# Causal attention weighed in gangs of four heads, one chunk at a time into four PSUM quadrants

## The chip, the cores and the metric

The kernel runs on one core of a Trainium2 chip. The metric is the device time of one execution in microseconds. It uses five engines: TensorE (PE; its weight loads are PEld), VectorE (DVE), ScalarE (ACT), GpSimd (POOL), and SyncE (SP), which issues the DMAs. TensorE's clock is granted at one of two levels, 1.2 or 2.4 GHz, which the profile shows as 0.5 and 1.0.

## The reference

The input is `x` of 8 x 512 x 128 in float32. Four blocks with residuals follow each other: causal attention with ALiBi (16 heads of 8 channels), a gated feed-forward network of 384 hidden channels, a second attention that works on selected and compressed keys, and the same feed-forward network again.

```python
# first attention, per sample: x is 512 x 128, 16 heads of 8
qkv = layernorm(x) @ w_qkv.T + b_qkv
scores = einsum('bhqd,bhkd->bhqk', q, k) / sqrt(8)
scores = scores + where(k <= q, -(q - k), -1e30)
probs = softmax(scores, axis=-1)
out = einsum('bhqk,bhkd->bhqd', probs, v)
x = x + out @ w_out.T + b_out
x = x + (silu(h @ wg.T) * (h @ wu.T)) @ wd.T          # h = layernorm(x), weights int32 / 127
# second attention: full 512 x 512 softmax per head gives the importance of each token
#   (entropy, maximum, influence); 51 tokens are gathered, 64 groups of 8 are compressed;
#   the 115 keys and values of each head are then attended to
x = x + attention_b(layernorm(x)) ; x = x + ffn(layernorm(x))
```

The change is in the line `out = einsum(...)` of the first attention and in the exponentials ahead of it.

## The kernel before, in words

The eight samples go through a pipeline of passes, `one_pass(i, a, p, m, s)`. In one pass four stages work on different samples side by side: `p` projects queries, keys and values of sample i+1; `a` is the causal attention and feed-forward network of sample i; `m` computes the full softmax of the second attention of sample i-1 and selects its keys; `s` attends with the small key set and runs the last feed-forward network of sample i-2. There are eleven passes. The first has `p` alone; the next has `a` and `p`; the next `a`, `p` and `m`; five in a hardware loop have all four; one has all but `p`; two more drain the pipeline. The causal attention `a` is in eight of them, in six of these beside both `m` and `s`. Each pass ends in a barrier of all engines.

Inside a pass the order of every engine's instructions is written out by hand in steps `n` from 0 to 74. In each of the first 64 steps `m` takes one 128 x 512 tile of the full scores: PE multiplies (`full_scores`, issued one step ahead), DVE finds the maximum (L947), ACT exponentiates (L747) and takes a logarithm (L750), POOL computes a threshold (L606), DVE sums an entropy two steps later (L902), and DVE or ACT scales the probabilities six steps later (L919, L693), which POOL adds up (L580).

The changed part of `a` stands in steps 20 to 49 (`A2_AT` to `A2_END`). Its scores are recomputed with the row maximum subtracted, transposed: keys in partitions, queries in columns. A head has four key tiles of 128; their widths are 512, 384, 256 and 128 because of causality, and they are packed into three units (`TILES`, `WIDTH`): one of 512, one of 384 + 128, one of 256. So there are 48 units `u` in a pass, in the steps that `a2_tiles(n)` gives, five units in every three steps. For each unit PE writes the scores and a mask into bank 3 or 4 alternately (`causal_minus_max`, L1165 and L1167), ACT takes the exponential into the probability buffer `pT` (L776), and PE multiplies the probabilities with the head's eight value columns and a column of ones (`weigh`, L1183). That product has nine rows; it goes to the quadrant of bank 5 that belongs to the head modulo four (`QROWS` 32, `HPQ` 4). A matmul in float32 is two records in the profile. After four heads ACT copies bank 5 out (`leave`, L686) and PE transposes it (`turn`, L1216). Unit `u` = 3 x head + chunk: one head's three chunks, then the next head's. `weigh(u - 3)` follows `causal_minus_max(u)`.

The small second attention has the same form: `weigh_hh` (L1197) writes head after head into the quadrants of bank 5, sometimes two heads in one step. The full scores (L1229) read partitions 64 and up of the same stacks from which the causal scores read the lower ones.

Of the kernel before, what the change touches and what calls it, by code (L numbers as in the profile page):

```python
# [9 lines left out]
BF16 = mybir.dt.bfloat16  # L10
# [3 lines left out]
P = 128  # L14
# [8 lines left out]
def hybrid_block(nc, x, w_qkv, b_qkv, w_out, b_out, wq_b, wk_b, wv_b, wo_b, w_gate, w_up, w_down, out):  # L23
    B, T, D = x.shape
# [15 lines left out]
    AL = 4  # L40
# [8 lines left out]
    with ExitStack() as ctx:  # L49
# [56 lines left out]
        kst = [k_stacks[64 * s:64 * s + 64, :, :] for s in range(2)]  # L106
        nm = [sb(f"nm{s}", [P, NT, H]) for s in range(2)]
        qsm = sb("qsm", [64, H, T], BF16)
        nmf = [sb(f"nmf{s}", [H, T]) for s in range(2)]
        nmr = [sb(f"nmr{s}", [H, T]) for s in range(2)]  # L110
        nmp = [sb(f"nmp{s}", [H, 3, T], BF16) for s in range(2)]
        vA = sb("vA", [P, NT, H, HD + 1])
        pT = [sb(f"pT{i}", [P, sum(WIDTH)]) for i in range(2)]
        ov = sb("ov", [P, T])
        rzo = [sb(f"rzo{s}", [P, NT, 4]) for s in range(2)]
        o = [sb(f"o{s}", [P, NT, P]) for s in range(2)]
# [25 lines left out]
        vrden = sb("vrden", [L, H])  # L142
        NE = 8
        E = setup[:, :].rearrange("p (n t) -> p n t", n=NE)
        alibi = sb("alibi", [1, AL + 1, T], BF16)
        junk = sb("junk", [P, T])
        nmB = sb("nmB", [P, H, NT])
        Z = sb("Z", [P, H, NT])
# [287 lines left out]
        def a1_before(u):  # L436

            return max([v + 1 for v in range(u) if a1_bank(v) == a1_bank(u)], default=0)

        def a2_tiles(n):  # L440

            return [u for u in range(3 * H) if A2_AT + (3 * u) // 5 == n]
# [19 lines left out]
        def one_pass(i, a, p, m, s):  # L462
            with nc.Block() as block:
# [176 lines left out]
                def _(act):  # L640
# [37 lines left out]

                    def leave(k, g):

                        act.wait_ge(s_pv[k], HPQ * (g + 1) * (1 if k else 3))
                        if g:
                            act.wait_ge(s_tv[k], g)
                        elif k == 0 and s:
                            act.wait_ge(s_tv[1], H // HPQ)
                        act.activation(ov[:, :], bank[5][:, :], ACT.Copy).then_inc(s_ov[k], 1)  # L686
# [51 lines left out]
                    for n in range(STEPS):  # L738
# [26 lines left out]
                        if a:  # L765
                            if n == S2_AT:
                                max_high(0)
                            if n == S2_AT + 2:
                                max_mid(0)

                            for u in a2_tiles(n):
                                h, c = u // 3, u % 3
                                if h >= 2:
                                    act.wait_ge(s_pv[0], u - 5)
                                act.wait_ge(s_s2[0], u + 1)
                                act.activation(pT[h % 2][:, c * T:c * T + WIDTH[c]], bank[3 + u % 2][:, 0:WIDTH[c]],  # L776
                                               ACT.Exp).then_inc(s_p[0], 1)
                        if m:

# [58 lines left out]
                def _(dve):  # L838
# [103 lines left out]
                    for n in range(STEPS):  # L942
# [159 lines left out]
                        if p:  # L1102
# [5 lines left out]
                            if n == P_TAIL + 7:  # L1108

                                dve.wait_ge(s_proj[0], 3)  # L1110
                                if a:
                                    dve.wait_ge(s_pv[0], 3 * H)
                                for t in range(NT):
                                    last = dve.tensor_tensor(
                                        vA[:, t, :, 0:HD],
                                        bank[5][:, t * P:(t + 1) * P].rearrange("p (h d) -> p h d", d=HD),
                                        bv[:, :].rearrange("p (h d) -> p h d", d=HD), ALU.add)
                                last.then_inc(s_vt[0], 1)

                @block.tensor  # L1120
                def _(pe):
# [33 lines left out]
                        last.then_inc(s_mt[k], 1)  # L1155

                    def causal_minus_max(u):
                        h, parts = u // 3, TILES[u % 3]
                        if u >= 2:
                            pe.wait_ge(s_p[0], u - 1)  # L1160
                        elif s:
                            pe.wait_ge(s_p[1], H)
                        for k, at in parts:
                            w = T - k * P
                            pe.matmul(bank[3 + u % 2][:, at:at + w], kst[0][0:A_MX, h, k * P:(k + 1) * P],  # L1165
                                      qst[0][0:A_MX, h, k * P:T], start=True, stop=True)
# [1 line left out]
                                             start=False, stop=True, skip_group_check=True)  # L1168
                        last.then_inc(s_s2[0], 1)

                    def weigh(u):

                        h, c = u // 3, u % 3
                        pe.wait_ge(s_p[0], u + 1)
                        if h >= HPQ and h % HPQ == 0:
                            pe.wait_ge(s_ov[0], h // HPQ)
                        if h == 0 and s:
                            pe.wait_ge(s_ov[1], H // HPQ)
                        elif h == 0:
                            pe.wait_ge(s_ma[0], 1)  # L1180
                        q = QROWS * (h % HPQ)
                        for k, at in TILES[c]:
                            last = pe.matmul(bank[5][q:q + HD + 1, k * P:T], vA[:, k, h, :],  # L1183
                                             pT[h % 2][:, c * T + at:c * T + at + T - k * P], start=(k == 0),
                                             stop=True, skip_group_check=(k > 0))
                        last.then_inc(s_pv[0], 1)

                    def weigh_hh(h):
# [113 lines left out]
                    for n in range(STEPS):  # L1302
# [123 lines left out]
                        if a:  # L1426
                            if n == A2_AT:
                                pe.wait_ge(s_mrow[0], DMA)
                            for u in a2_tiles(n):
                                causal_minus_max(u)  # L1430
                                if u > 2:
                                    weigh(u - 3)
                            if n == A2_END:
                                for u in range(3 * H - 3, 3 * H):
                                    weigh(u)
                            if n in TURN_AT[0]:
                                turn(0, TURN_AT[0].index(n))
                            if n == A_TAIL:
# [75 lines left out]
```

## Time and profile before

| | |
|---|---|
| median of 3 runs | 2352.26 us (2349.68 to 2664.49) |
| span of the profiled execution | 2347.5 us, 25009 instructions |
| PE busy | 1731.0 us, 74% |
| DVE busy | 1492.3 us, 64% |
| ACT busy | 1121.6 us, 48% |
| POOL busy | 892.7 us, 38% |
| DMA, main queue | 57.57 MB, 15.1% of 16 engines |
| L1183, weighing | 1024 records |
| L776, exponentials | 384 |

The profiled execution has no time of its own beside its span, which lies 2.2 us below the fastest run and 4.8 us below the median. Busy time is a sum over stages with different limits, so the share of the whole span says little; the rows below are by stage. In the timeline a record's length includes a part in which the next record already runs, so the time that an operation holds PE is read from its start to the start of what follows.

### The profile page before, as it was taken

The numbers are of one execution on the slowest core, as the hardware profiler recorded it, in microseconds if no ns is written. First come the engines' busy times: TensorE is split into PE (matmuls) and PEld (weight loads), VectorE is DVE, ScalarE is ACT, GpSimd is POOL, SyncE is SP. The second block draws the span as 40 slices with busy tenths as digits, with TensorE's granted clock in tenths as the row PEclk, the third lists the DMA queues.
The fourth block names the chain that finished last, engine by engine and source line by source line (L and its number), as shares of the span: only waits on it lengthen the run. The fifth ranks groups of instructions, "written<-read, shape, count | busy, mean of one in ns | idle before, by whom it ended". The sixth has DMA issues, their size and how long they took to land. (4 is left out here: it accounts for less than half of the span.)

```text
span 2347.5 us, 25009 instructions
## 1 busy us (share of the span) xinstructions
PE 1731.0 (74%) x6733; PEld 734.6 (31%) x6733; DVE 1492.3 (64%) x3701; ACT 1121.6 (48%) x2726; POOL 892.7 (38%) x1252
## 2 busy tenths in 40 slices
PE   1686479668986799568976799668977799647537
PEld 1222233333333332333334332433334332322122
DVE  0401388847886677757875677757876677647931
ACT  1033167516772277416672376516672377446603
POOL 2001146513553155514562154514562155425700
PEclk9998559756987599756987589756987589656557
DMA  3002300250004200240005100240005100130010
GB/s 61 13 2 37 53 2 1 38 75 4 1 5 87 29 3 1 50 69 4 1 12 84 24 3 1 46 72 4 1 5 90 20 3 1 24 51 1 5 24 5
DMA packets 64106, 59.35 MB, mean 25 GB/s; under 512 B 10400, under 2 KB 61648, under 8 KB 63952
## 3 DMA queue, kind: packets, MB, share of 16 engines
q1 hardware_dynamic: 63952, 57.57, 15.1%
q8 instruction: 63, 1.03, 0.2%
q14 instruction: 91, 0.75, 0.1%
HBM read 39.10 MB, written 18.27 MB: 24 GB/s over the span
## 5 line engine op out<-in xcount | busy, mean ns | idle before, releaser
L580 POOL TENSOR_TENSOR psum<-psum,setup 128x512 f32<-128x512 f32 x480 | 614.1, 1279 | 55.5 <-ACT setup L693 52.1
L947 DVE TENSOR_REDUCE nmB<-bank 128x1 f32<-128x512 f32 x512 | 348.2, 680 | 290.7 <-PE bank L1229 289.8
L747 ACT ACTIVATE setup<-bank,nmB 128x512 f32<-128x512 f32 x512 | 349.8, 683 | 283.4 <-DVE nmB L947 252.7
L606 POOL TENSOR_TENSOR thr<-lnZ,nmB 128x1 f32<-128x1 f32 x512 | 102.1, 199 | 790.3 <-ACT lnZ L750 786.9
L902 DVE SCALAR_TENSOR_TENSOR junk<-bank,thr,setup 128x512 f32<-128x512 f32 x512 | 378.6, 739 | 20.5 <-POOL thr L606 18.8
L1229 PE MATMUL bank<-k_stacks,q_stacks 48*128 48x512 bf16 x512 | 236.8, 470 | 181.1 <-DMA k_stacks<-part_dram 111.0
L1183 PE MATMUL bank<-pT,vA 128*9 128x512 f32 (+3 forms) x1024 | 342.4, 440 | 10.8 <-ACT ov L686 10.6
L866 DVE TENSOR_REDUCE nm<-bank 128x1 f32<-128x512 f32 (+3 forms) x512 | 225.6, 482 | 127.6 <-PE bank L1148 124.7
L1145 PE MATMUL bank<-k_stacks,q_stacks 52*128 52x512 bf16 (+3 forms) x512 | 217.4, 425 | 120.0 <-PEq L1476 59.2
L776 ACT ACTIVATE pT<-bank 128x512 f32<-128x512 f32 (+1 forms) x384 | 198.8, 521 | 190.9 <-PE bank L1167 188.8
L919 DVE TENSOR_SCALAR setup<-setup,rz 128x512 f32<-128x512 f32 x288 | 195.0, 677 | 0.0
L1229 PEld LDWEIGHTS bank<-k_stacks,q_stacks 48*128 48x128 bf16 x512 | 47.7, 96 | 418.5 <-DVE junk L902 167.7
L1165 PE MATMUL bank<-q_stacks,k_stacks 55*128 55x512 bf16 (+3 forms) x512 | 159.8, 312 | 21.4 <-ACT pT L776 11.9
L1148 PE MATMUL bank<-maskqk,identb 128*128 128x128 bf16 x512 | 143.3, 280 | 0.0
L693 ACT ACTIVATE setup<-setup,rz 128x512 f32<-128x512 f32 x192 | 135.6, 706 | 0.0
L1197 PE MATMUL bank<-p,vsm 115*9 115x512 f32 x256 | 124.6, 722 | 4.4 <-ACT ov L686 3.6
L1167 PE MATMUL bank<-maskkq,identb 128*128 128x128 bf16 x512 | 118.6, 232 | 0.0
L750 ACT ACTIVATE lnZ<-Z 128x1 f32<-128x1 f32 x512 | 103.9, 203 | 16.2
L875 DVE RECIPROCAL rzo<-bank 128x16 f32<-128x16 f32 x64 | 16.3, 254 | 146.6 <-PE bank L1216 146.6
L1145 PEld LDWEIGHTS bank<-k_stacks,q_stacks 52*128 52x128 bf16 x512 | 51.9, 101 | 182.4 <-issue 90.9
L763 ACT ACTIVATE p<-bank 115x512 f32<-115x512 f32 x128 | 72.2, 584 | 66.5 <-PE bank L1397 33.8
L747 ACT ACTIVATION_READ_ACCUMULATOR setup<-bank,nmB 128x1 f32 x512 | 101.7, 199 | 0.0
(184 smaller groups left out, 2370.5 us busy)
## 6 DMA issues: line engine op xcount, KB each, us to landing
part_dram<-part SPq DMA_DIRECT2D x16, 768.0 KB, 3.3
q_stacks<-part_dram SPq DMA_DIRECT2D x96, 128.0 KB
k_stacks<-part_dram SPq DMA_DIRECT2D x96, 128.0 KB
qsm<-part_dram SPq DMA_DIRECT2D x48, 128.0 KB
x<-in_L_attn_a_x_dram SPq DMA_DIRECT2D x8, 256.0 KB, 3.9
x_dram<-x SPq DMA_DIRECT2D x8, 256.0 KB, 10.2
x2s<-x_dram SPq DMA_DIRECT2D x8, 256.0 KB, 11.4
out_dram<-x SPq DMA_DIRECT2D x8, 256.0 KB, 2.3
```

What stands on the lines that cost most here:

```text
L580: pool.tensor_tensor(psum[:, :], psum[:, :], E[:, n % NE, :], ALU.add).then_inc(s_bi, 1)
L747: act.activation(E[:, n % NE, :], RING[n % RN][:, :], ACT.Exp, bias=nmB[:, h, t:t + 1], accum_out=Z[:, h, t:t + 1]).then_inc(s_be, 1)
L776: act.activation(pT[h % 2][:, c * T:c * T + WIDTH[c]], bank[3 + u % 2][:, 0:WIDTH[c]], ACT.Exp).then_inc(s_p[0], 1)
L866: last = dve.tensor_reduce(nm[0][:, t, h:h + 1], bank[a1_bank(u)][:, at:at + (t + 1) * P], AX_X, ALU.max, negate=True)
L902: dve.scalar_tensor_tensor(out=junk[:, :], in0=RING[n % RN][:, :], scalar=thr[:, h, t:t + 1], in1=E[:, n % NE, :], op0=ALU.max, op1=ALU.mu ...
L919: dve.tensor_scalar(E[:, n % NE, :], E[:, n % NE, :], rz[:, h, t:t + 1], None, ALU.mult).then_inc(s_scv, 1)
L947: dve.tensor_reduce(nmB[:, h, t:t + 1], RING[n % RN][:, :], AX_X, ALU.max, negate=True).then_inc(s_bm, 1)
L1145: pe.matmul(bank[a1_bank(u)][:, at:at + (t + 1) * P], qst[0][0:A_SC, h, t * P:(t + 1) * P], kst[0][0:A_SC, h, 0:(t + 1) * P], start=True, ...
L1148: last = pe.matmul(bank[a1_bank(u)][:, at + t * P:at + (t + 1) * P], identb[:, :], maskqk[:, :], start=False, stop=True, skip_group_check= ...
L1165: pe.matmul(bank[3 + u % 2][:, at:at + w], kst[0][0:A_MX, h, k * P:(k + 1) * P], qst[0][0:A_MX, h, k * P:T], start=True, stop=True)
L1183: last = pe.matmul(bank[5][q:q + HD + 1, k * P:T], vA[:, k, h, :], pT[h % 2][:, c * T + at:c * T + at + T - k * P], start=(k == 0), stop=T ...
L1229: pe.matmul(RING[n % RN][:, :], qst[1][0:B_SC, h, t * P:(t + 1) * P], kst[1][0:B_SC, h, :], start=True, stop=True).then_inc(s_bs, 1)
```

## The change

Unit `u` now stands for another tile. `gang_tile(u)` gives head `4 * (u // 12) + u % 4` and chunk `u // 4 % 3`: the first chunk of four heads, then the second chunk of the four, then the third. There are four probability buffers instead of two, one for each head of a gang. A weighing unit is now a chunk of a gang (12 in a pass instead of 48): for each key tile of the chunk four matmuls, one for each quadrant of bank 5, then one increment of the semaphore. All waits on it are rescaled. To make room, the two maxima buffers `nmf` and `nmr` are shared between the two attentions, and the constant rows `alibi` lie in the setup tile.

```diff
--- before.py
+++ after.py
@@ -106,11 +106,11 @@
         kst = [k_stacks[64 * s:64 * s + 64, :, :] for s in range(2)]
         nm = [sb(f"nm{s}", [P, NT, H]) for s in range(2)]
         qsm = sb("qsm", [64, H, T], BF16)
-        nmf = [sb(f"nmf{s}", [H, T]) for s in range(2)]
-        nmr = [sb(f"nmr{s}", [H, T]) for s in range(2)]
+        nmf = [sb("nmf", [H, T])] * 2
+        nmr = [sb("nmr", [H, T])] * 2
         nmp = [sb(f"nmp{s}", [H, 3, T], BF16) for s in range(2)]
         vA = sb("vA", [P, NT, H, HD + 1])
-        pT = [sb(f"pT{i}", [P, sum(WIDTH)]) for i in range(2)]
+        pT = [sb(f"pT{i}", [P, sum(WIDTH)]) for i in range(4)]
         ov = sb("ov", [P, T])
         rzo = [sb(f"rzo{s}", [P, NT, 4]) for s in range(2)]
         o = [sb(f"o{s}", [P, NT, P]) for s in range(2)]
@@ -142,7 +142,7 @@
         vrden = sb("vrden", [L, H])
         NE = 8
         E = setup[:, :].rearrange("p (n t) -> p n t", n=NE)
-        alibi = sb("alibi", [1, AL + 1, T], BF16)
+        alibi = setup[0:1, 22 * P:].bitcast(BF16).rearrange("p (a t) -> p a t", a=AL + 1)
         junk = sb("junk", [P, T])
         nmB = sb("nmB", [P, H, NT])
         Z = sb("Z", [P, H, NT])
@@ -437,6 +437,10 @@
 
             return max([v + 1 for v in range(u) if a1_bank(v) == a1_bank(u)], default=0)
 
+        def gang_tile(u):
+
+            return HPQ * (u // (3 * HPQ)) + u % HPQ, u // HPQ % 3
+
         def a2_tiles(n):
 
             return [u for u in range(3 * H) if A2_AT + (3 * u) // 5 == n]
@@ -678,7 +682,7 @@
 
                     def leave(k, g):
 
-                        act.wait_ge(s_pv[k], HPQ * (g + 1) * (1 if k else 3))
+                        act.wait_ge(s_pv[k], (g + 1) * (HPQ if k else 3))
                         if g:
                             act.wait_ge(s_tv[k], g)
                         elif k == 0 and s:
@@ -769,11 +773,11 @@
                                 max_mid(0)
 
                             for u in a2_tiles(n):
-                                h, c = u // 3, u % 3
-                                if h >= 2:
-                                    act.wait_ge(s_pv[0], u - 5)
+                                h, c = gang_tile(u)
+                                if h >= HPQ:
+                                    act.wait_ge(s_pv[0], u // HPQ - 2)
                                 act.wait_ge(s_s2[0], u + 1)
-                                act.activation(pT[h % 2][:, c * T:c * T + WIDTH[c]], bank[3 + u % 2][:, 0:WIDTH[c]],
+                                act.activation(pT[h % HPQ][:, c * T:c * T + WIDTH[c]], bank[3 + u % 2][:, 0:WIDTH[c]],
                                                ACT.Exp).then_inc(s_p[0], 1)
                         if m:
 
@@ -1109,7 +1113,7 @@
 
                                 dve.wait_ge(s_proj[0], 3)
                                 if a:
-                                    dve.wait_ge(s_pv[0], 3 * H)
+                                    dve.wait_ge(s_pv[0], 3 * H // HPQ)
                                 for t in range(NT):
                                     last = dve.tensor_tensor(
                                         vA[:, t, :, 0:HD],
@@ -1155,12 +1159,12 @@
                         last.then_inc(s_mt[k], 1)
 
                     def causal_minus_max(u):
-                        h, parts = u // 3, TILES[u % 3]
+                        h, c = gang_tile(u)
                         if u >= 2:
                             pe.wait_ge(s_p[0], u - 1)
                         elif s:
                             pe.wait_ge(s_p[1], H)
-                        for k, at in parts:
+                        for k, at in TILES[c]:
                             w = T - k * P
                             pe.matmul(bank[3 + u % 2][:, at:at + w], kst[0][0:A_MX, h, k * P:(k + 1) * P],
                                       qst[0][0:A_MX, h, k * P:T], start=True, stop=True)
@@ -1168,21 +1172,21 @@
                                              start=False, stop=True, skip_group_check=True)
                         last.then_inc(s_s2[0], 1)
 
-                    def weigh(u):
-
-                        h, c = u // 3, u % 3
-                        pe.wait_ge(s_p[0], u + 1)
-                        if h >= HPQ and h % HPQ == 0:
-                            pe.wait_ge(s_ov[0], h // HPQ)
-                        if h == 0 and s:
+                    def weigh(w):
+
+                        g, c = w // 3, w % 3
+                        pe.wait_ge(s_p[0], HPQ * (w + 1))
+                        if c == 0 and g:
+                            pe.wait_ge(s_ov[0], g)
+                        elif c == 0 and s:
                             pe.wait_ge(s_ov[1], H // HPQ)
-                        elif h == 0:
+                        elif c == 0:
                             pe.wait_ge(s_ma[0], 1)
-                        q = QROWS * (h % HPQ)
                         for k, at in TILES[c]:
-                            last = pe.matmul(bank[5][q:q + HD + 1, k * P:T], vA[:, k, h, :],
-                                             pT[h % 2][:, c * T + at:c * T + at + T - k * P], start=(k == 0),
-                                             stop=True, skip_group_check=(k > 0))
+                            for j in range(HPQ):
+                                last = pe.matmul(bank[5][QROWS * j:QROWS * j + HD + 1, k * P:T], vA[:, k, HPQ * g + j, :],
+                                                 pT[j][:, c * T + at:c * T + at + T - k * P], start=(k == 0),
+                                                 stop=True, skip_group_check=(k > 0))
                         last.then_inc(s_pv[0], 1)
 
                     def weigh_hh(h):
@@ -1428,11 +1432,10 @@
                                 pe.wait_ge(s_mrow[0], DMA)
                             for u in a2_tiles(n):
                                 causal_minus_max(u)
-                                if u > 2:
-                                    weigh(u - 3)
+                                if u >= HPQ and u % HPQ == 1:
+                                    weigh(u // HPQ - 1)
                             if n == A2_END:
-                                for u in range(3 * H - 3, 3 * H):
-                                    weigh(u)
+                                weigh(3 * H // HPQ - 1)
                             if n in TURN_AT[0]:
                                 turn(0, TURN_AT[0].index(n))
                             if n == A_TAIL:
```

PE in the middle of the stage, pass of the hardware loop, before. `pT` are probability buffers, `vA` values; `k_stacks` and `q_stacks` hold the parts of keys and queries; bank 5 collects the weighed heads, banks 0, 1, 2 and 6 take full scores.

```order
L1165 MATMUL bank3<-q_stacks,k_stacks 128x512 [waits probabilities0]
L1167 MATMUL bank3<-maskkq,identb 128x128
L1183 MATMUL bank5<-pT1,vA 9x512 [waits probabilities0]
L1229 MATMUL bank6<-k_stacks,q_stacks 128x512 [waits entropy_sums]
L1165 MATMUL bank4<-q_stacks,k_stacks 128x384 [waits probabilities0]
L1167 MATMUL bank4<-maskkq,identb 128x128
L1165 MATMUL bank4<-q_stacks,k_stacks 128x128
L1167 MATMUL bank4<-maskkq,identb 128x128
L1183 MATMUL bank5<-pT1,vA 9x384 [waits probabilities0]
L1183 MATMUL bank5<-pT1,vA 9x128
L1165 MATMUL bank3<-q_stacks,k_stacks 128x256 [waits probabilities0]
L1167 MATMUL bank3<-maskkq,identb 128x128
```

The same place after the change:

```order
L1233 MATMUL bank2<-k_stacks,q_stacks 128x512 [waits entropy_sums]
L1169 MATMUL bank4<-q_stacks,k_stacks 128x384 [waits probabilities0]
L1171 MATMUL bank4<-maskkq,identb 128x128
L1169 MATMUL bank4<-q_stacks,k_stacks 128x128
L1171 MATMUL bank4<-maskkq,identb 128x128
L1187 MATMUL bank5<-pT0,vA 9x512 [waits four_heads_out_of_psum0,probabilities0]
L1187 MATMUL bank5<-pT1,vA 9x512
L1187 MATMUL bank5<-pT2,vA 9x512
L1187 MATMUL bank5<-pT3,vA 9x512
L1233 MATMUL bank6<-k_stacks,q_stacks 128x512 [waits entropy_sums]
L1169 MATMUL bank3<-q_stacks,k_stacks 128x384 [waits probabilities0]
L1171 MATMUL bank3<-maskkq,identb 128x128
```

One head's weighing stood behind each unit of scores. Now four heads' weighing stands together behind the second of four units of scores; the three units between have none.

ACT at the same steps, before:

```order
L747 ACTIVATE setup,Z<-bank1,nmB 128x512 [waits influences,entropy_sums,full_maxima]
L750 ACTIVATE lnZ<-Z 128x1 [waits full_exponentials]
L776 ACTIVATE pT1<-bank4 128x256 [waits scores_minus_max0,heads_weighted0]
L747 ACTIVATE setup,Z<-bank2,nmB 128x512 [waits influences,entropy_sums,full_maxima]
L750 ACTIVATE lnZ<-Z 128x1 [waits full_exponentials]
L776 ACTIVATE pT0<-bank3 128x512 [waits scores_minus_max0,heads_weighted0]
L776 ACTIVATE pT0<-bank4 128x512 [waits scores_minus_max0,heads_weighted0]
```

and after:

```order
L751 ACTIVATE setup,Z<-bank1,nmB 128x512 [waits influences,entropy_sums,full_maxima]
L754 ACTIVATE lnZ<-Z 128x1 [waits full_exponentials]
L780 ACTIVATE pT1<-bank4 128x512 [waits scores_minus_max0,heads_weighted0]
L751 ACTIVATE setup,Z<-bank2,nmB 128x512 [waits influences,entropy_sums,full_maxima]
L754 ACTIVATE lnZ<-Z 128x1 [waits full_exponentials]
L780 ACTIVATE pT2<-bank3 128x512 [waits scores_minus_max0,heads_weighted0]
L780 ACTIVATE pT3<-bank4 128x512 [waits scores_minus_max0,heads_weighted0]
```

The exponentials stand in the same steps between those of the full scores; their buffer, and at some places their width, differ.

## Rows read from the trace of the kernel before

**Rows 1.** The page, part 2: granted clock of TensorE, tenths of full speed, 40 slices

```profile
PEclk9998559756987599756987589756987589656557
```

**Rows 2.** Busy time by stage: start:end, length, each engine (x instructions), clock, DMA

```profile
123.90:192.80 68.90, 67.86 (x258) 20.51 (x259) 1.53 (x6) 26.46 (x51) 0.00 (x0) 1.00 0.00 1
344.50:412.10 67.60, 66.03 (x280) 20.16 (x281) 55.26 (x125) 49.55 (x135) 42.11 (x59) 0.96 0.00 1
1116.90:1195.40 78.50, 74.58 (x313) 24.58 (x313) 62.05 (x138) 56.23 (x143) 40.82 (x59) 1.00 0.00 1
1382.40:1463.80 81.40, 77.49 (x313) 24.78 (x314) 61.99 (x139) 56.24 (x143) 40.78 (x59) 0.96 0.00 1
```

**Rows 3.** Waits in 1116.9 to 1195.4: who waited for whom, us, times, longest

```profile
DVE nmB L947 <- PE bank L1229: 13.3, 14, 2.3
```

**Rows 4.** Busy time by stage of line L1183, the weighing, alone

```profile
1116.90:1195.40 78.50, 39.35 (x119) 7.27 (x120) 1.00 0.00 1
```

**Rows 5.** Timeline of PE: start us, length us, instruction, tiles; high clock, full pass

```profile
1144.57 1.03 PE L1183 MATMUL bank<-pT,vA 128*9 128x512 f32 x2
...
1145.53 0.33 PE L1165 MATMUL bank<-q_stacks,k_stacks 55*128 55x384 bf16 x1
...
1146.33 1.03 PE L1183 MATMUL bank<-pT,vA 128*9 128x384 f32 x4
1147.29 0.39 PE L1229 MATMUL bank<-k_stacks,q_stacks 48*128 48x512 bf16 x1
...
1147.77 0.60 PE L1183 MATMUL bank<-pT,vA 128*9 128x256 f32 x2
1148.30 0.39 PE L1165 MATMUL bank<-q_stacks,k_stacks 55*128 55x512 bf16 x1
```

**Rows 6.** Timeline of PE, weighing L1197 of the other attention, low and high clock

```profile
1090.62 1.88 PE L1197 MATMUL bank<-p,vsm 115*9 115x512 f32 x4
1092.44 0.60 PE L1229 MATMUL bank<-k_stacks,q_stacks 48*128 48x512 bf16 x1
...
1095.24 1.03 PE L1197 MATMUL bank<-p,vsm 115*9 115x512 f32 x2
1096.20 0.39 PE L1229 MATMUL bank<-k_stacks,q_stacks 48*128 48x512 bf16 x1
...
1099.30 1.16 PE L1197 MATMUL bank<-p,vsm 115*9 115x512 f32 x4
1100.40 0.66 PE L1216 MATMUL bank<-identf,ov 128*128 128x128 f32 x4
```

**Rows 7.** Timeline of ACT, the probabilities that L1197 weighs

```profile
1098.32 1.06 ACT L763 ACTIVATE p<-bank 115x512 f32<-115x512 f32 x2
```

**Rows 8.** Timeline of PE in the first attention pass, low clock

```profile
125.65 0.60 PE L1165 MATMUL bank<-q_stacks,k_stacks 55*128 55x512 bf16 x1
...
126.41 1.88 PE L1183 MATMUL bank<-pT,vA 128*9 128x512 f32 x2
128.22 0.50 PE L1165 MATMUL bank<-q_stacks,k_stacks 55*128 55x384 bf16 x1
...
129.31 1.88 PE L1183 MATMUL bank<-pT,vA 128*9 128x384 f32 x4
...
131.66 1.02 PE L1183 MATMUL bank<-pT,vA 128*9 128x256 f32 x2
132.62 0.61 PE L1165 MATMUL bank<-q_stacks,k_stacks 55*128 55x512 bf16 x1
```

**Rows 9.** Busy time by stage, with the granted clock (PEclk)

```profile
1051.00:1083.00 32.00, 28.19 (x103) 12.03 (x102) 27.28 (x66) 14.18 (x39) 7.73 (x14) 0.50 0.02 4
1098.00:1116.00 18.00, 14.64 (x52) 3.89 (x51) 11.74 (x31) 17.76 (x44) 11.38 (x16) 1.00 0.01 2
1181.00:1219.00 38.00, 30.22 (x126) 13.69 (x125) 29.64 (x82) 27.16 (x65) 21.81 (x32) 0.96 0.03 8
1199.80:1206.60 6.80, 3.13 (x15) 1.25 (x13) 6.77 (x17) 2.23 (x8) 4.49 (x6) 1.00 0.00 0
```

## The prediction

> **What bounds the kernel now.** I read the page first, then the stage that is changed, pass by pass, then its waits, then single instructions. The kernel is eleven passes in a row, and the changed stage (scores minus maximum on TensorE, exponential on ScalarE, weighing on TensorE) stands once in each of eight. The page's clock line [rows 1] shows TensorE's granted clock alternating between its levels; the nines lie where this stage lies. The table by stage [rows 2] shows the stage in the first attention pass (only this work), in the second, and in a full pass; the four other full passes not shown last 78.5 to 78.6 us. In a full pass TensorE (PE) is busy 74.58 of 78.5 us, VectorE (DVE) 62.05, ScalarE 56.23. DVE waits 13.3 us for PE's full scores [rows 3], queued behind the gang's work. The rest of DVE's idle time is 78.5 - 62.05 - 13.3 = 3.15 us. So PE sets the stage, and DVE is next; ScalarE and GpSimd (40.82) have more room. Steps are written out in one order and everything behind the stage follows it, so a shorter stage shortens the pass.
>
> **Weighing, before.** It has 39.35 us of PE in a stage [rows 4]. At the high clock one head's three chunks hold PE from 1144.57 to 1145.53, 1146.33 to 1147.29 and 1147.77 to 1148.30 [rows 5]: 0.96 + 0.96 + 0.53 = 2.45 us, 9.8 us for four heads. At the low clock [rows 8]: 1.81, 1.81 (same busy time, 1.88, in both rows) and 0.96, so 4.58 us a head.
>
> **Weighing, after.** The same matmuls, the four quadrants in turn. Does a second quadrant run beside the first? The profile already has such a pair, in the other attention's weighing: alone, 1095.24 to 1096.20, 0.96 us; two heads in neighbouring quadrants, 1099.30 to 1100.40, 1.10 us; at the low clock the pair takes 1090.62 to 1092.44, 1.82 us [rows 6], as much as a single one of 1.81 [rows 8]. So an added quadrant costs 0.01 to 0.14 us. The 0.14 is no cost of the array: ScalarE finishes the second head's probabilities at 1099.38 [rows 7], 0.08 after the first head had begun. In the changed kernel all four heads are ready, since the weighing waits for the fourth. Chunk 0 of four heads is then 0.96 + 3 x (0.01 to 0.14) = 0.99 to 1.38 us, chunk 1 (two groups of four) 1.02 to 1.80, chunk 2 0.56 to 0.95: 2.6 to 4.1 us a gang. I take 2.7, near the pair at the low clock. At the low clock 2 x 1.84 + 0.99 = 4.7. A stage saves 4 x (9.8 - 2.7) = 28.4 us of PE at the high clock.
>
> The Trainium skill (TensorE: Matmul & The Clock Gate, Part 3, on packing small matmuls) gives three column tiles 2.38 times one. Estimated from that page, four would give about 3.2 times, and 39.35 / 3.2 = 12.3 us a stage instead of 10.8; by it the sum changes by 1.5 us of PE a stage. No run here shows four.
>
> **Other edits.** Scores go four heads a chunk instead of three chunks a head: same matmuls, same two banks. ScalarE's exponentials are the same; their wait is for a weighing three units back, which PE has issued two tiles earlier, covered by the scores between. The weighing waits for the tile that the scores issued just before it waited for, so it adds no wait; behind it at most 1.4 us of PE stand before the next full scores, covered by the one step that these run ahead. PE's wait for the four heads' evacuation goes (1.5 us a stage at most, inside PE's 3.9 us of idle time); the next gang's weighing comes four tiles later. At the end one gang's chunk remains instead of three units: under 1 us. Sharing the two small maxima buffers costs nothing: their uses lie some six steps apart. Two more probability buffers, and the constant rows laid into the setup tile, move no work and no DMA. I cost these at zero; if the cover fails, 1 us a stage.
>
> **The clock.** This decides the size. The granted clock [rows 9]: 0.50 in 1051 to 1083 although PE is busy 28.2 of 32 us, with short matmuls; 1.00 in 1098 to 1116 at 14.6 of 18; and it falls at the end of 1199.8 to 1206.6, after PE had been busy 3.1 of 6.8. The changed stage takes 28.4 us of the densest PE work out: 74.58 - 28.4 = 46 us of PE in about 65, 71%, and less in the stretches with no gate, up or transpose. The first attention pass enters its stage at the low clock [rows 8], as single weighings of 1.88 us show (the clock column has 1.00 for the whole stage, but the durations are plain), and it left it under long weighings that now are a quarter. So both levels are priced.
>
> High clock, full pass: DVE sets it, 62.05 + 3.15 = 65.2 us, 13.3 less than 78.5. Low clock: PE's other work, 74.58 - 39.35 = 35.2 us, stretches. A short pair of scores goes from 0.80 (1145.53 to 1146.33, [rows 5]) to 1.09 (128.22 to 129.31, [rows 8]), x1.4; long ones at most x2. I take x1.65: 58 + 4 x 4.7 = 77 us, 2 less than now (bounds 68 to 89: 10 less to 11 more). That is PE-bound again.
>
> Second attention pass: high 55.3 + 3.15 = 58.4 against 67.6, 9 less; low 27 x 1.65 + 19 = 63, 4 less. First attention pass: high, 28.4 less of 68.9; low, a head's scores are 6.97 - 4.58 = 2.39 us (125.65 to 132.62, [rows 8]), a gang 9.6 + 4.7 = 14.3, the stage 57 and 2 for transposes: 10 less.
>
> **The sum.** I take about half of each full stage at either level: (65.2 + 77) / 2 = 71, 7.5 less. Six passes: 45. Second pass 6, first pass 15 (starts low). Behind the stage PE is busy 30.2 of 38 us at 0.96 [rows 9]; entering at the low clock costs about 1 us in each of eight passes, since dense gate products follow. 45 + 6 + 15 - 8 = 58 us off the profiled 2347.5, so 2289.5. The median of the runs, 2352.26, stands 4.8 above the profiled span; on its scale 2294. (One of the three runs took 2664; I predict the undisturbed time.)
>
> **Rivals.**
> *The clock holds throughout (0.20).* For it: 1098 to 1116 stays at 1.00 with DVE idle a third of the time and two weighings overlapped. Against: the added idle time. 6 x 13.3 + 9 + 28 = 117: 2235.
> *The clock is low in every one of these stages (0.20).* For: 1051 to 1083 shows a busy PE left at 0.50. Against: gates and projections fall into the stage. 6 x 2 + 4 + 10 - 8 = 18: 2334. The Trainium skill (TensorE: Matmul & The Clock Gate, Part 1, on the clock gate) says that the default state is throttled and that activity releases it; by that rule taking wall time of matmuls away can cost the clock. The trace agrees as far as the fall after 1206.6; by the rule the time would be the 2334 here.
> *Slower (0.07): the low clock outlasts the stage.* The 38 us behind it, with 30.2 of PE, become 30.2 x 1.65 = 50, 12 more in each of eight passes: 96 - 26 = 70 more, 2422. It is slower by 2% once the stretch behind stays low in six of the eight. Against: dense gate and down products stand in that stretch.
> *Four quadrants don't overlap in this kernel (0.06),* because the second half of each float32 product must wait for its own weights. PE work is as before, minus the short waits: about 2345. Against: the pair.
>
> **How the numbers follow.** Forecast (mixed clock) 0.47, its own range 2265 to 2320. A measurement of this kernel tells about 2% from no change, 2305 on the fast side. Seven tenths of the forecast's case lie below that: 0.33, and with the held clock 0.53 faster. Same: 0.14 + 0.20 + 0.05 = 0.39. Slower 0.08. Range 2236 to 2345: it takes in both clock cases, without the farther half of the held clock and the last two rivals.
>
> **What would show it.** Right: rows of weighing in which eight or sixteen records of one chunk take about 1.0 us at the high clock; PE's busy time in a full pass's stage 45 to 60; the stage 66 to 76 us long; granted clock between 0.5 and 1.0 in it; DVE waiting for full scores under 10 us. Wrong: a chunk of four at 2 us or more (no overlap); clock 1.00 and the stage near 65 (first rival); clock 0.5 and the stage near 77 (second); the stretch behind the stage longer (third).

## The result: 1.5% faster, and the profile after

The change takes 2320.1 us (median of 3 runs, 2299.72 to 2322.49) against 2352.26: ratio 0.985, 95% interval 0.980 to 0.990. The same kernel was run twice more, beside other runs of the kernel before: 2308.4 us, ratio 0.978 (0.972 to 0.985), and 2306.1 us, ratio 0.983 (0.977 to 0.989). The forecast was 2294 us, with 2236 to 2345 as its range. The three sets put the gain at 1.5, 2.2 and 1.7%, around the 2% from which the prediction calls it faster. (Executions disturbed from outside are left out of all ratios; of the gangs of two below, 2298.5 and 2315.0 us are left, and their profile is of one left out.)

Of the page of the kernel after, these lines answer to [rows 1] and to the groups of costliest instructions. L1187 is the weighing (L1183 before), L951 the maximum of the full scores (L947), L1171 the mask product (L1167).

```profile
span 2320.8 us, 24897 instructions
PE 1737.5 (75%) x6733; PEld 741.3 (32%) x6733; DVE 1501.2 (65%) x3701; ACT 1114.8 (48%) x2726; POOL 894.2 (39%) x1252
PEclk9996555655766565656566576656566565655557
L951 DVE TENSOR_REDUCE nmB<-bank 128x1 f32<-128x512 f32 x512 | 348.1, 680 | 267.3 <-PE bank L1233 266.9
L1187 PE MATMUL bank<-pT,vA 128*9 128x512 f32 (+3 forms) x1024 | 147.9, 697 | 1.5 <-ACT pT L780 1.5
```

The same 1024 weighing records hold PE for 147.9 us; the page before had 342.4. Those 194.5 us are gone from the weighing, and yet PE's total rose from 1731.0 to 1737.5 us. The clock line says why: the nines of [rows 1] are fives, sixes and sevens. Its mean over the span fell from 0.757 to 0.634. (The nines at the start of both lines can't be trusted: in the first attention pass the column shows 0.9 to 1.0 where single records have their low-clock lengths, as the timeline below shows.)

The table by stage, of two full passes (fourth and sixth of those with attention). A stage is counted from the start of its first exponential (L780) to the start of its last. Columns as in [rows 2]: start and end, length, PE, PEld, DVE, ACT, POOL, clock.

```profile
834.30:914.40 80.10, 76.41 (x315) 24.42 (x314) 63.02 (x138) 55.35 (x143) 40.48 (x57) 0.53 0.00 1
1363.10:1434.20 71.10, 65.04 (x315) 22.97 (x314) 62.08 (x139) 54.92 (x143) 41.09 (x59) 0.70 0.00 1
```

And of the second run of the same kernel:

```profile
1098.60:1166.30 67.70, 60.39 (x315) 21.81 (x314) 59.28 (x137) 54.68 (x143) 41.40 (x57) 0.77 0.00 1
1608.00:1688.10 80.10, 76.43 (x315) 24.42 (x315) 63.01 (x137) 55.27 (x143) 40.55 (x57) 0.53 0.00 1
```

Identical instructions take 67.7 us in one pass and 80.1 in another pass of the same execution, and what differs is the granted clock. Over the 18 full-pass stages of three profiled executions, seven last 80.1 to 80.8 us at 0.52 or 0.53, one 73.5 at 0.66, seven 70.8 to 71.2 at 0.70 or 0.71, three 67.7 to 68.2 at 0.76 or 0.77. The mean is 74.2 us at 0.64; before it was 79.0 at 0.99. From one execution to the next the mean of the six stages differs too: 77.6, 71.4 and 73.6 us at 0.58, 0.70 and 0.66. Means of one execution that lie inside these ranges can't be told from the change. Why one pass gets more clock than the next is not known. At 0.53 the stage is 1.6 us longer than the undisturbed 78.5 of before.

Where the time went in such a low-clock stage, by line: the groups of PE in 1116.9 to 1195.4 before,

```profile
L1183 PE MATMUL bank<-pT,vA 128*9 128x512 f32 (+3 forms) x119 | 39.6, 435 | 1.5 <-ACT ov L686 1.5
L1165 PE MATMUL bank<-q_stacks,k_stacks 55*128 55x384 bf16 (+3 forms) x63 | 19.2, 305 | 1.8 <-ACT pT L776 1.8
L1167 PE MATMUL bank<-maskkq,identb 128*128 128x128 bf16 x63 | 14.4, 229 | 0.0
L1229 PE MATMUL bank<-k_stacks,q_stacks 48*128 48x512 bf16 x28 | 10.8, 387 | 0.0
```

and in 834.3 to 914.4 after:

```profile
L1169 PE MATMUL bank<-q_stacks,k_stacks 55*128 55x384 bf16 (+3 forms) x63 | 26.7, 424 | 1.4 <-ACT pT L780 1.4
L1187 PE MATMUL bank<-pT,vA 128*9 128x512 f32 (+3 forms) x120 | 18.3, 734 | 0.0
L1171 PE MATMUL bank<-maskkq,identb 128*128 128x128 bf16 x63 | 17.8, 282 | 0.0
L1233 PE MATMUL bank<-k_stacks,q_stacks 48*128 48x512 bf16 x29 | 16.5, 568 | 0.0
```

The weighing fell by 21 us of PE in the stage (39.35 by [rows 4] to 18.31), PE's other work rose from 35.2 to 58.1 us. The net is +1.8 us of PE in 80.1 us. In the 67.7 us stage weighing is 14.4 us and the rest 46.0. DVE's wait for the full scores, 13.3 us in [rows 3], is 12.6 at the low clock (1616.3 to 1696.5) and 5.0 in the 67.7 us stage of the second run:

```profile
DVE nmB L951 <- PE bank L1233: 12.6, 9, 3.6
```

```profile
DVE nmB L951 <- PE bank L1233: 5.0, 4, 1.8
```

So DVE still waits for PE in both; no stage that was read this way ran at DVE's own pace.

The overlap itself is complete. PE's timeline (start, length, instruction), first the low clock in the first attention pass, then the high clock at 1411 us:

```profile
127.34 1.90 PE L1187 MATMUL bank<-pT,vA 128*9 128x512 f32 x8
129.17 0.50 PE L1169 MATMUL bank<-q_stacks,k_stacks 55*128 55x384 bf16 x1
...
132.66 1.90 PE L1187 MATMUL bank<-pT,vA 128*9 128x384 f32 x16
134.49 0.39 PE L1169 MATMUL bank<-q_stacks,k_stacks 55*128 55x256 bf16 x1
134.81 0.29 PE L1171 MATMUL bank<-maskkq,identb 128*128 128x128 bf16 x1
...
1411.27 0.23 PE L1171 MATMUL bank<-maskkq,identb 128*128 128x128 bf16 x1
1411.43 1.05 PE L1187 MATMUL bank<-pT,vA 128*9 128x384 f32 x16
1412.41 0.66 PE L1220 MATMUL bank<-identf,ov 128*128 128x128 f32 x4
```

A chunk of four heads holds PE for 1.83 us at the low clock (1.81 for one head, [rows 8]) and 0.98 at the high (0.96 for one, [rows 5]). Three added quadrants cost 0.02 us together; the first records of the four start 6 to 7 ns apart.

### The profile page after: what moved, and what is told of

It is laid out like the page before. It is cut to its first block and busy times, and to the rows that moved or that the text cites. A ratio compares the mean times of both kernels' runs of the same rounds, so it can differ in the third digit from the quotient of the medians.

```text
span 2320.8 us, 24897 instructions
## 1 busy us (share of the span) xinstructions
PE 1737.5 (75%) x6733; PEld 741.3 (32%) x6733; DVE 1501.2 (65%) x3701; ACT 1114.8 (48%) x2726; POOL 894.2 (39%) x1252
## 3 DMA queue, kind: packets, MB, share of 16 engines
q1 hardware_dynamic: 63952, 57.57, 14.4%
## 5 line engine op out<-in xcount | busy, mean ns | idle before, releaser
L951 DVE TENSOR_REDUCE nmB<-bank 128x1 f32<-128x512 f32 x512 | 348.1, 680 | 267.3 <-PE bank L1233 266.9
L1233 PE MATMUL bank<-k_stacks,q_stacks 48*128 48x512 bf16 x512 | 276.2, 548 | 176.1 <-DMA k_stacks<-part_dram 97.4
L906 DVE SCALAR_TENSOR_TENSOR junk<-bank,thr,setup 128x512 f32<-128x512 f32 x512 | 378.5, 739 | 16.4 <-POOL thr L610 14.4
L780 ACT ACTIVATE pT<-bank 128x512 f32<-128x512 f32 (+1 forms) x384 | 192.7, 520 | 174.8 <-PE bank L1171 173.5
L1169 PE MATMUL bank<-q_stacks,k_stacks 55*128 55x384 bf16 (+3 forms) x512 | 212.0, 414 | 23.9 <-ACT pT L780 14.5
L923 DVE TENSOR_SCALAR setup<-setup,rz 128x512 f32<-128x512 f32 x288 | 206.9, 719 | 0.0
L1187 PE MATMUL bank<-pT,vA 128*9 128x512 f32 (+3 forms) x1024 | 147.9, 697 | 1.5 <-ACT pT L780 1.5
L1171 PE MATMUL bank<-maskkq,identb 128*128 128x128 bf16 x512 | 142.3, 278 | 0.0
L1201 PE MATMUL bank<-p,vsm 115*9 115x512 f32 x256 | 136.1, 789 | 3.5 <-ACT ov L690 2.9
```

Source lines behind the costliest of these rows:

```text
L780: act.activation(pT[h % HPQ][:, c * T:c * T + WIDTH[c]], bank[3 + u % 2][:, 0:WIDTH[c]], ACT.Exp).then_inc(s_p[0], 1)
L906: dve.scalar_tensor_tensor(out=junk[:, :], in0=RING[n % RN][:, :], scalar=thr[:, h, t:t + 1], in1=E[:, n % NE, :], op0=ALU.max, op1=ALU.mu ...
L923: dve.tensor_scalar(E[:, n % NE, :], E[:, n % NE, :], rz[:, h, t:t + 1], None, ALU.mult).then_inc(s_scv, 1)
L951: dve.tensor_reduce(nmB[:, h, t:t + 1], RING[n % RN][:, :], AX_X, ALU.max, negate=True).then_inc(s_bm, 1)
L1187: last = pe.matmul(bank[5][QROWS * j:QROWS * j + HD + 1, k * P:T], vA[:, k, HPQ * g + j, :], pT[j][:, c * T + at:c * T + at + T - k * P], ...
L1201: pe.matmul(bank[5][q:q + HD + 1, :], vsm[0:NK, h, :], p2[h % 2][0:NK, :], start=True, stop=True).then_inc(s_pv[1], 1)
```

## The experiments

Theory: packing saves PE's time as computed, the granted clock falls with it, and the lower clock slows everything else on PE. Rivals: the new order or the buffers cost the time; the low clock has nothing to do with the weighing; PE's busy time, of any kind, holds the clock. The means below are over the six full passes of one profiled execution each.

### The order alone

Gang order and four buffers, but each head's chunk weighed by itself, three units behind its scores:

```diff
-                                if u >= HPQ and u % HPQ == 1:
-                                    weigh(u // HPQ - 1)
+                                if u > 2:
+                                    weigh(u - 3)
```

> The order of tiles and the four buffers of the change, but each head's weighing alone behind its unit of scores, as before. Clock theory (the overlap frees PE time, the lower granted clock takes most of it back): PE's work and its clock as before, the stage 77 to 80 us at clock 1.00 in a full pass, time 2340 to 2360. Rival, the order and not the clock is what counts (whatever the change gained or lost comes from it): stage as in the changed kernel, 2300 to 2325, or, if the order costs, over 2370.

Measured 2365.3 us, ratio 1.007 (1.003 to 1.010), 5 us above the expected range. The stage in the middle of the hardware loop:

```profile
1125.40:1204.70 79.30, 75.62 (x315) 24.82 (x315) 60.96 (x139) 56.46 (x144) 41.78 (x59) 1.00 0.00 1
```

The clock is as before, at 1.00, and the stage 0.8 us longer than 78.5; so are three more of the six. (The other two are 80.7 at 0.98 and 84.6 at 0.92; the mean is 80.4 at 0.98. The profiled execution is the slowest of ten, 2388.5 us.) So order and buffers bring no gain, and they do not lower the clock to that of the change; they cost 0.7%. Gain and clock loss come with the packed weighing. Packing does two things at once: four heads run side by side, and the weighing stands in one bunch instead of behind every unit. Bunches without overlap were not run, so which of the two takes the clock is not shown.

### Gangs of two

```diff
+        GANG = 2
-            return HPQ * (u // (3 * HPQ)) + u % HPQ, u // HPQ % 3
+            return GANG * (u // (3 * GANG)) + u % GANG, u // GANG % 3
...
-                            for j in range(HPQ):
+                            for h in range(h0, h0 + GANG):
```

> Gangs of two heads: two quadrants in turn instead of four. Weighing holds PE about 8 x 2.6 = 21 us of a stage at the high clock instead of 10.8 with four and 39 with one. Clock theory: the granted clock in the stage lies clearly above the 0.53 of four, the stage is 66 to 74 us, time 2260 to 2305, faster than four heads although it saves less PE time. Rival, PE's work is all that counts at whatever clock: between the kernel before and the change, 2320 to 2350.

Here `h0` is the first head of the gang. The median of all four executions is 2328.1 us; by the two that the ratio counts it is 0.981 (0.972 to 0.990). The change has 0.978 to 0.985 in its three sets. One stage of the profiled execution (2339.4 us):

```profile
1639.20:1710.60 71.40, 65.41 (x318) 22.67 (x317) 60.65 (x136) 55.11 (x144) 41.39 (x57) 0.88 0.00 1
```

Mean clock 0.82, mean stage 73.2 us. With one head (the first experiment), two and four (the change) side by side the mean clock of the stage is 0.98, 0.82 and 0.64, the mean stage 80.4, 73.2 and 74.2 us. Two heads save less of PE's time and lose less of the clock, and the time comes out the same within the noise. Stage and clock came as expected; the time, faster than four heads, was not shown. This is support for the theory and no proof, since the one profile is of an execution that the ratio leaves out. The mean clock over the whole span points the same way: 0.67 and 0.70 in the two counted executions, 0.61 to 0.67 in the 14 of the change.

### More work, to get the clock back

Three kinds of useless work were added to the change. The first issues each gang's first key tile twice, into the same place:

```diff
-                            for j in range(HPQ):
+                            for j in list(range(HPQ)) * (2 if k == 0 else 1):
```

> The change, with the first key tile's weighing of each gang issued twice (the second writes the same values again): 4 x 0.9 us more PE work in a stage at the high clock, 4 x 1.7 at the low one. Clock theory: the added dense work raises the clock for part of the stage, time 2285 to 2325. Rival, PE's work is all that counts: 4 x 1.7 x 8 = 54 us more than the change, about 2370.

The second doubles every causal score product:

```diff
-                            pe.matmul(bank[3 + u % 2][:, at:at + w], kst[0][0:A_MX, h, k * P:(k + 1) * P],
-                                      qst[0][0:A_MX, h, k * P:T], start=True, stop=True)
+                            for _ in range(2):
+                                pe.matmul(bank[3 + u % 2][:, at:at + w], kst[0][0:A_MX, h, k * P:(k + 1) * P],
+                                          qst[0][0:A_MX, h, k * P:T], start=True, stop=True)
```

> The change, with each matmul of scores minus maximum issued twice (the second writes the same values again), the mask once: 16 x 0.5 = 8 us more PE work in a stage at the high clock, 17 at the low one. Clock theory: PE is busier between its waits, the clock is granted for most of the stage, which is then set by DVE at 66 to 74 us: 2265 to 2320. Rival, PE's work is all that counts: 17 x 8 = 136 us more than the change, about 2450.

Doubled weighing: 2311.1 us, ratio 0.984 (0.976 to 0.991), 32 more records in a stage, and the best stages so far apart from the three fastest of the change:

```profile
573.70:642.80 69.10, 58.94 (x347) 22.17 (x346) 59.86 (x138) 54.71 (x144) 41.90 (x58) 0.88 0.00 1
```

PE has more work and is *less* busy (58.9 us against 65.0 in the change's stage at 0.70), since all of it runs faster at the higher clock. The mean clock is 0.81. The time is inside the expected range. Doubled scores: 2353.8 us, ratio 1.001 (0.996 to 1.006). The clock rises too, to 0.76, but PE's work with it, to 70.2 us a stage, and the stage is 76.4. Neither of its two expected results (2265 to 2320, about 2450) came.

Then the change once more, the doubled weighing once more, short matmuls as a control, and both repeats together.

> The changed kernel as it is, beside the others of this call. Both theories: 2300 to 2325; it is the yardstick for the next three.

> The kernel x3_double_first again, to settle its sign against the change. Clock theory, by its trace (full stages of 69 us at clock 0.85 to 0.88, two of six over 70): 10 to 30 us below b1_change_again. Rival, PE's work is all that counts: 50 us above it.

The short matmuls:

```diff
+                        if c == 0:
+                            for _ in range(4):
+                                pe.matmul(bank[5][0:HD + 1, 0:16], vA[:, 0, HPQ * g, :], pT[0][:, 0:16], start=True, stop=True)
```

> The change, with four float32 matmuls of 16 columns ahead of each gang's first chunk, whose output the weighing then overwrites. A pair of records of such a matmul held PE 0.45 us at the low clock, so it adds about as much PE time as the repeated weighing of b2_double_again (1.7 us a gang at the low clock), but in short pieces. Clock theory, in the form that dense work and not PE time brings the clock: clock in the stage as in the change, 0.50 to 0.65, and 20 to 60 us above b1_change_again. Rival, any added work or any shift in time does what b2 does: as b2_double_again.

Both repeats together: the doubled first key tile, and the score products of each gang's first chunk twice (`range(2 if c == 0 else 1)`).

> b2_double_again, and in the four units of chunk 0 of each gang the matmul of scores is also issued twice, where the stage has the least dense work: 16 x 0.21 = 3.4 us more PE work at the high clock, 58 in all, still under DVE's 62. Clock theory: the clock is held for nearly the whole stage (over 0.9), the stage is 65 to 69 us, 2260 to 2300, the fastest so far. Rival, more PE work only costs: 30 us above b2_double_again.

| kernel | us (median) | ratio to before | stage | clock | PE in stage | ahead | behind |
|---|---|---|---|---|---|---|---|
| before | 2355.0 | 1 | 79.0 | 0.99 | 75.1 | 118.0 | 64.0 |
| the change | 2308.4 | 0.978 (0.972 to 0.985) | 71.5 | 0.70 | 65.4 | 119.7 | 64.5 |
| first key tile twice | 2318.2 | 0.986 (0.981 to 0.991) | 72.5 | 0.79 | 64.4 | 121.2 | 64.8 |
| short matmuls | 2328.9 | 0.989 (0.983 to 0.996) | 73.7 | 0.67 | 68.2 | 119.5 | 65.0 |
| both repeats | 2290.2 | 0.977 (0.971 to 0.982) | 71.2 | 0.85 | 63.8 | 116.9 | 64.3 |

Ahead and behind are the us from the pass's start to the stage and from the stage to the pass's end. These two and the stage, its clock and PE's work in it are means of one profiled execution; that of the short matmuls is 21 us faster than their median.

The repeats of long matmuls put the stage's clock at 0.79 and 0.85, above all three means of the change (0.58 to 0.70); with the short ones it is 0.67. The mean clock over the whole span, averaged over all counted executions, agrees: 0.64 for the change (14 executions), 0.65 with the short matmuls (5), 0.68 with the doubled weighing (10) and 0.69 with both repeats (12, with the next set). The short matmuls are a weak control. They were expected to hold PE for 0.45 us each; all four of a gang together hold it for about 0.2 us, so they add about 1 us to a stage where the doubled weighing adds four times that. Whether the kind of work or its amount brings the clock back is not shown. By the medians they cost 20 us, at the edge of the noise.

The doubled weighing lost its expectation on the time: 10 us above the change instead of 10 to 30 below. Its stages average 71.8 us over two profiles, 2.4 less than the change's 74.2, but the part ahead of the stage is 121.4 us against 118.3 (in some passes the small attention's first scores start 25 to 32 us into the pass instead of 22.4, when its keys have come back by DMA). Whether the repeats cause that was not tried; it stays open. In this set both repeats gained little in the stage either (71.2 against 71.5): 17 of the 22 us between the two profiled executions lie ahead of it (2.8 us in each of six passes). Over all profiles the stage does get shorter: 70.9 us with both repeats (two profiles), 74.2 with the change (three).

A last set, to settle whether both repeats beat the change, whether the scores' repeat does it alone, and whether more helps (the first key tile three times):

> The changed kernel once more, beside the next three. 2295 to 2325; its six full stages between 67 us at clock 0.77 and 80 at 0.53, in no fixed order of the passes.

> The kernel b4_double_both again, to see whether it beats the change. Clock theory: full stages of 69 to 73 us at 0.84 to 0.88, none at 80, time 10 to 25 us below d1_change_third. Rival, what it gains in clock it pays in PE work: within 8 us of d1.

> Of the two repeats in d2 only the scores of chunk 0. If the stretch with chunk 0 is where the clock is lost, it holds the clock as d2 does (0.8 and over) with 3.9 us less PE work a stage: 67 to 71 us a stage, 2275 to 2295. If both are needed, clock 0.6 to 0.75 and a time as d1.

> d2 with the first key tile weighed three times: another 3.9 us of PE work at the high clock, 62 in all, equal to DVE's. Clock theory: clock over 0.9 but nothing left to gain, stage 69 to 73, time as d2 or up to 15 us above. If PE work alone counts, 4 x 1.8 x 8 = 58 us above d2.

| kernel | us (median) | ratio to before | stage | clock | PE in stage |
|---|---|---|---|---|---|
| the change | 2306.1 | 0.983 (0.977 to 0.989) | 73.6 | 0.65 | 68.1 |
| both repeats | 2282.5 | 0.973 (0.967 to 0.978) | 70.7 | 0.86 | 63.1 |
| scores' repeat alone | 2318.6 | 0.985 (0.980 to 0.991) | 73.5 | 0.72 | 66.6 |
| three times, and scores' repeat | 2311.2 | 0.986 (0.981 to 0.991) | 73.4 | 0.87 | 66.0 |

A stage of both repeats, and one of the last kernel:

```profile
1600.10:1670.10 70.00, 62.68 (x362) 23.24 (x360) 57.43 (x139) 54.73 (x143) 42.23 (x59) 0.87 0.00 1
```

```profile
1859.30:1934.60 75.30, 67.81 (x394) 23.69 (x392) 58.34 (x138) 54.86 (x143) 42.17 (x59) 0.85 0.01 1
```

At nearly the same clock the second has 32 more records, 5.1 us more of PE, and is 5.3 us longer: past this point added work buys no clock and is paid in full. The means in the table say the same: 0.86 and 0.87, 2.9 us more of PE, 2.7 us more of stage. So does the mean clock over the whole span, 0.69 with either kernel, while the medians are 29 us apart. The 29 us lie between the two results expected of it (up to 15 us, and 58 if PE's work alone counts). The scores' repeat alone has a clock of 0.72 and the time of the change within the noise, the result expected if both repeats are needed.

Both repeats came out 24 us below the change beside them, within the 10 to 25 expected, with no stage at 80 us. Over both sets the 12 counted executions with both repeats average 2288.9 us and the 11 of the change 2304.9, ratio 0.993 with an interval of 0.989 to 0.997. The version with 47 useless matmul records a stage is the fastest kernel of this study, 2.3% and 2.7% below the kernel before. The clock did not reach the 0.9 that was expected of it at first.

## Why the prediction came out as it did

**The overlap: right.** Predicted 0.01 to 0.14 us for each added quadrant; measured under 0.01 (0.02 for three). A gang is 2.5 us at the high clock (2.7 taken) and 4.6 at the low (4.7 taken). The rival without overlap is refuted. The Trainium skill (TensorE: Matmul & The Clock Gate, Part 3, on packing small matmuls) measures 2.38 times for three column tiles, from which an estimate of 3.2 for four was drawn; here four heads take 0.98 us instead of 4 x 0.96, 3.9 times, and the measurement decides.

**The other edits: too low.** They were costed at zero, or 1 us a stage if a cover fails. The order alone costs 0.8 us in a typical stage, but 0.7% of the whole program (13 us between the medians), and where the rest of that falls was not located.

**The clock: the mechanism right, its share mis-sized.** The time fell inside the range, and the term of the sum that was mis-sized is "about half of each full stage at either level". In three profiles the mean granted clock of the six full stages is 0.58, 0.70 and 0.65; 0.64 is 28% of the time at the high level, not half. Seven of 18 stages are almost wholly low. With 28% the prediction's own two prices give 73.7 us for the stage, and 74.2 was measured. That this fits so well is partly luck: the low-clock price is 3 us too low (next paragraph), and a stage at 0.77 is 2.9 us shorter than the prices make it (67.7 against 70.6). The first experiment shows that the loss comes with the packed weighing (side by side and in bunches) and not with order or buffers, and the repeats show that part of it can be had back with more long matmuls. The rule cited in the prediction from the Trainium skill (TensorE: Matmul & The Clock Gate, Part 1, on the clock gate), that activity releases the throttle, fits that. PE's busy share alone doesn't tell the clock: PE was busy 76.4 of 80.1 us at 0.53, and 75.6 of 79.3 at 1.00 with unpacked weighing. Which property of the work counts was not isolated.

**The low-clock price: 3 us too low.** The stretched work was right to 0.1 us (58 predicted, 58.1 measured; weighing 18.8 and 18.3), and PE's busy time of 76.4 was right. But the stage was set equal to it. It also holds 3.7 us in which PE waits, as before (78.5 - 74.58 = 3.9), so the low stage is 80.1, not 77: a loss of 1.6, not a gain of 2. The high-clock value of 65.2, with DVE as the bound, was never reached, and no stage had the high clock throughout; the three fastest stages are 67.7 to 68.2 at 0.76 and 0.77, and DVE still waits 5 us for PE there.

**The rest of the sum,** by the mean of the three profiles (2309.7 us, 37.8 below the profiled 2347.5): the six full stages gave 6 x 4.8 = 29 where 45 was predicted, the second pass's 3 instead of 6, the first pass's 10 instead of 15. That stage takes 59.0 us, the low-clock value of the prediction, and it is at the low clock nearly throughout: its mask products (L1171) last 0.29 us each, against 0.23 at the high clock, though the clock column shows 0.90 to 1.00 there. Before the change they shortened to 0.23 us about 14 us into the stage. Behind the six full stages 3 us were lost (6 predicted), ahead of them 2 (0 predicted). Together 42 - 5 = 37 us, against 58 predicted. 16 of the 21 us missing are the full stages. The three medians, 2306 to 2320 us, lie at the slow end of the range that the prediction gave the mixed clock (2265 to 2320). Its likelier outcome (0.53), faster by more than 2%, did not come in the first set (0.985), and the two later ones (0.978, 0.983) stand close to that line.

**The rivals.** A held clock (2235) did not occur. Clock low everywhere (2334) is closest in the profiled execution of 2320.8, where four of six full stages are low, but not true as a rule. The low clock outlasting the stage (2422) is refuted: the stretch behind is 64.6 us against 64.0.

**What would show it:** a chunk of about 1.0 us came true, the clock between 0.5 and 1.0 too, the stage of 66 to 76 us as a mean and in 11 of 18; PE's 45 to 60 us did not (60 to 77), nor DVE's wait under 10 us where the clock is low.

## What to carry to other kernels

Small outputs in different quadrants ran side by side here at almost no cost (0.98 us for four, 0.96 for one), so packing was worth nearly its full factor in PE's time for the weighing; but count the granted clock as a term of the sum, for all work of PE around the packed part, not for the packed part alone. Here 21 to 25 us of PE saved in a stage cost 11 to 23 on everything else. Where the clock has dropped, compare passes with the same instructions, read more than one execution, and try whether a few repeated long matmuls bring it back before shortening PE further.

## What the runs showed of the hardware

- Stages with identical instructions last 67.7 and 80.1 us in one execution, their length falling steadily with the granted clock.
- PE busy 95% of a stage (76.4 of 80.1 us) at a granted clock of 0.53, and 95% at 1.00 with unpacked weighing (75.6 of 79.3).
- Forty-seven added matmul records a stage made the program 0.7% faster than the change; 32 more records made it 29 us slower again (2311.2 against 2282.5), slower than the change beside it (2306.1).
- Not only quadrants overlap. A full-scores product (keys at partitions 64 and up) and a causal one (partitions 0 to 54) start in the same 10 ns, before the change (at 1194.80 and 1194.81 us) and after it:

```profile
1381.99 0.39 PE L1233 MATMUL bank<-k_stacks,q_stacks 48*128 48x512 bf16 x1 [0.34 <-DVE junk L906]
1381.99 0.39 PE L1169 MATMUL bank<-q_stacks,k_stacks 55*128 55x512 bf16 x1
```
